# Attention's loop over head pairs in a fused two-layer kernel: a hardware loop written out as 32 iterations with constant waits

## What is computed

```
x = x + cross_attention(layernorm(x), ctx)      # 16 heads of 128, q and k normalised per head
x = x + hadamard_ffn(layernorm(x))              # 512 -> 2 x 2048 -> 512
x = x + state_space_mix(ctx, layernorm(x))      # scan over 512 values, 16 states
x = x + moe_ffn(layernorm(x))                   # 16 experts, two of them for each token, and a shared one
```

```
q = rmsnorm(xn @ Wq[:, h]) * gq;  k = rmsnorm(c @ Wk[:, h]) * gk;  v = c @ Wv[:, h]
out[:, h] = softmax(q @ k.T / sqrt(128)) @ v
x += out @ Wo
```

## Time and profile before

| | us |
|---|---|
| median of 3 runs | 2648.81 |
| lowest, highest | 2648.68, 2650.52 |
| span of the profiled execution, first to last instruction | 2643.4 |
| median less that span | 5.4 |
| attention in that span | 107.5 to 1272.9, behind a start of attention from about 80 |

### The profile page before, as it was taken

One profiled execution on the slowest core, in us unless ns is written; L12 is line 12 of the kernel. 1 busy time (PEld: TensorE's weight loads), 2 busy tenths in 40 slices (PEclk: granted clock), 3 DMA queues, 4 the chain that ended last, 5 costly groups with the idle time before them and its releaser, 6 DMA issues. The chain is left out here.

```text
span 2643.4 us, 35123 instructions
## 1 busy us (share of the span) xinstructions
PE 2284.0 (86%) x10784; PEld 1760.5 (67%) x10785; DVE 1797.4 (68%) x3239; ACT 1279.1 (48%) x2275; POOL 1356.7 (51%) x1104
## 2 busy tenths in 40 slices
PE   3699999999999999999693899998998869578980
PEld 2688888888887888887442666665665547456770
DVE  6466777768677777876683998898988966312323
ACT  2344454444454444544383866757766632223430
POOL 0232333323333333333293988989979941488324
PEclk8799999999999999999886999999999988789995
DMA  7513232122322232211348565555565321665317
GB/s 286 216 53 113 88 112 79 58 109 89 113 78 79 88 113 89 87 64 39 131 166 265 168 208 204 175 185 187 196 183 183 123 84 48 215 219 173 117 52 266
DMA packets 136761, 363.49 MB, mean 138 GB/s; under 512 B 21264, under 2 KB 58768, under 8 KB 118416
## 3 DMA queue, kind: packets, MB, share of 16 engines
q1 hardware_dynamic: 123504, 328.30, 36.1%
q0 software_dynamic: 6320, 20.71, 2.4%
q10 hardware_dynamic: 6768, 12.32, 1.2%
HBM read 289.99 MB, written 71.30 MB: 137 GB/s over the span
## 5 line engine op out<-in xcount | busy, mean ns | idle before, releaser
L641 POOL TENSOR_SCALAR att_probs<-att_probs,att_recip 128x512 f32<-128x512 f32 x256 | 181.8, 713 | 562.6 <-DVE att_recip L708 562.6
L1819 POOL TENSOR_TENSOR mix_drive<-mix_du,mix_rows 128x512 f32<-128x512 f32 x256 | 326.6, 1282 | 48.8 <-DVE mix_state L1891 15.9
L565 ACT ACTIVATE att_probs<-att_s,att_bias,att_rq 128x512 f32<-128x512 f32 x256 | 200.6, 784 | 288.3 <-DVE att_bias L704 288.1
L1891 DVE TENSOR_TENSOR_SCAN mix_state<-mix_state,mix_drive 128x512 f32<-128x512 f32 x256 | 312.9, 1222 | 30.8 <-POOL mix_drive L1819 17.3
L1671 ACT ACTIVATE mix_state<-mix_delta,mix_a 128x512 f32<-128x512 f32 x256 | 175.8, 690 | 227.8 <-DVE mix_drive L1902 187.4
L1804 POOL TENSOR_TENSOR mix_y<-mix_y,mix_drive 128x512 f32<-128x512 f32 x180 | 230.6, 1281 | 46.0 <-DVE mix_drive L1902 45.8
L1580 PE MATMUL mix_down<-mix_wd,mix_hT 128*128 128x512 f32 x512 | 232.0, 596 | 8.8 <-DVE residual_x L1922 8.8
L703 DVE TENSOR_REDUCE att_nmax<-att_s 128x1 f32<-128x512 f32 x256 | 175.1, 684 | 71.4 <-PE att_s L101 64.6
L744 DVE TENSOR_TENSOR att_pT<-att_pt,att_pT 128x512 fp32r<-128x512 f32 x256 | 170.1, 686 | 66.0 <-ACT att_pT L571 61.9
L571 ACT CAST att_pT<-att_pt 128x512 fp32r<-128x512 f32 x256 | 144.2, 593 | 133.4 <-PE att_pt L422 129.2
L99 PE MATMUL att_w<-att_w_qkv,att_cx 128*128 128x256 f32 x512 | 158.7, 310 | 35.2 <-DVE att_w_qkv L690 26.5
(11 more groups left out here) (354 smaller groups left out, 6703.7 us busy)
## 6 DMA issues: line engine op xcount, KB each, us to landing
att_xn<-normT SPq DMA_DIRECT2D x32, 2048.0 KB, 8.7
mix_gu<-guT SPq DMA_DIRECT2D x64, 1024.0 KB, 8.2
mix_rows<-bc_d SPq DMA_DIRECT2D x128, 256.0 KB, 4.8
guT<-att_ffnT SPq DMA_DIRECT2D x32, 512.0 KB, 5.7
mix_wd<-wdT SPq DMA_DIRECT2D x16, 1024.0 KB, 7.9
slots<-exp_y ACTq DMA_DIRECT2D x47, 256.0 KB
normT<-nrm_outT SPq DMA_DIRECT2D x4, 2048.0 KB, 9.1
exp_raw<-in_L_ffn_Wg SPq DMA_DIRECT2D x16, 512.0 KB, 5.1
```

The costliest lines, as they stand in the source:

```text
L565: act.activation(probs[:, n, :], ps_s[n % 2][:, :], ACT.Exp, bias=bias[:, n:n + 1], scale=rq[:, n:n + 1], accum_out=sums[:, n:n + 1]).then ...
L641: pool.tensor_scalar(probs[:, n, :], probs[:, n, :], recip[:, n:n + 1], 1.0, ALU.mult, ALU.mult).then_inc(s_pn, 1)
L1819: pool.tensor_tensor(drive[q % RING][:, :], du[i % DUS][:, :], rows[g % ROWS][:, 0, :], ALU.mult).then_inc(s_drive, 1)
L1891: dve.tensor_tensor_scan(h[:, :], h[:, :], drive[q % RING][:, :], 0.0, ALU.mult, ALU.add).then_inc(s_scan, 1)
```

## The change

Both loops are replaced by plain Python loops, so that the code of all 32 iterations stands one behind the other on every engine. `hp` is a number everywhere: the tests for the last pair become `hp < PAIRS - 1`, every wait compares with a constant, and the computation of the step counter's base falls away. On POOL `wait_apart(...)` becomes `pool.wait_ge(...)`, and `s_pace` goes. The instructions that compute, their order, the DMAs and what each waits for stay as they are.

```diff
         def pairs(eng, iteration):
-            with eng.Fori(0, PAIRS - 1) as hp:
+            for hp in range(PAIRS):
                 for b in range(B):
-                    iteration(hp, b, False)
-            for b in range(B):
-                iteration(PAIRS - 1, b, b == B - 1)
+                    iteration(hp, b, hp == PAIRS - 1 and b == B - 1)
...
-                    if b == 0 and not (isinstance(hp, int) and hp == PAIRS - 1):
+                    if b == 0 and hp < PAIRS - 1:
                         sp.wait_ge(s_w, 2 * hp + 2)
                         load_weights(hp + 1)
...
-                    if not (isinstance(hp, int) and b >= B - 2):
+                    if hp < PAIRS - 1 or b < B - 2:
...
                 def norm_p(i, n):
-                    wait_apart(pool, s_rec, 8 * i + n + 1, s_pace)
+                    pool.wait_ge(s_rec, 8 * i + n + 1)
...
-                base = own.n
-                per_pair = B * (8 + 1) + 3
-                def iteration(own, hp, b, last):
+                def iteration(hp, b, last):
                     i = hp * B + b
                     j = i + 1
-                    more = not isinstance(hp, int)
+                    more = hp < PAIRS - 1
...
-                with dve.Fori(0, PAIRS - 1) as hp:
-                    own = Steps(dve, s_dve, hp * per_pair + base)
-                    for b in range(B):
-                        iteration(own, hp, b, False)
-                    assert own.n == per_pair, own.n
-                own = Steps(dve, s_dve, (PAIRS - 1) * per_pair + base)
-                for b in range(B):
-                    iteration(own, PAIRS - 1, b, b == B - 1)
+                pairs(dve, iteration)
```

More of the change, by code:

```diff
@@ L303, in stage_attention @@
         s_dve = m.sem("dve_steps")
-        s_pace = m.sem("pace")
         s_fraw, s_ft, s_fout = m.sem("ffn_raw_in"), m.sem("ffn_turned"), m.sem("ffn_turned_out")
@@ L644, in norm_k @@
                 def norm_k(j):
-                    wait_apart(pool, s_kss, j + 1, s_pace)
+                    pool.wait_ge(s_kss, j + 1)
                     pool.tensor_tensor(rk[:, :], kss[:, :], power[:, :], ALU.pow).then_inc(s_rk, 1)
                 def norm_q(j):
-                    wait_apart(pool, s_qss, j + 1, s_pace)
+                    pool.wait_ge(s_qss, j + 1)
                     pool.tensor_tensor(rq[:, :], qss[:, :], power[:, :], ALU.pow).then_inc(s_rq, 1)
@@ L653, in split_ffn @@
                     parts = [fT[:, n, :, :].rearrange("p k n -> p (k n)") for n in range(2)]
-                    wait_apart(pool, s_fout, i + 1, s_pace)
-                    wait_apart(pool, s_fst, 16 * (i + 1), s_pace)
+                    pool.wait_ge(s_fout, i + 1)
+                    pool.wait_ge(s_fst, 16 * (i + 1))
                     pool.tensor_scalar(parts[0], fraw[:, :], 1.0, 1.0, ALU.mult, ALU.mult).then_inc(s_fhi, 1)
-                    wait_apart(pool, s_fhi, i + 1, s_pace)
+                    pool.wait_ge(s_fhi, i + 1)
                     pool.tensor_tensor(parts[1], fraw[:, :], parts[0].bitcast(F32), ALU.subtract).then_inc(s_flo, 1)
```

## The result

| | before | changed |
|---|---|---|
| median of the 4 runs each of the first comparison, us | 2649.02 | 2624.35 |
| lowest, highest | 2648.68, 2650.52 | 2621.90, 2629.47 |
| ratio, 95% interval | | 0.9914 [0.9897, 0.9932] |
| the same, two later comparisons | | 0.9903 [0.9888, 0.9919], 0.9908 [0.9893, 0.9922] |
| span of the profiled execution | 2643.4 | 2627.7 |

A forecast was written before the change was run, and what follows sets the result against it. Attention was taken as bound by TensorE (PE busy 97%), which stands for code at six loop jumps, 3.5 us each. Median 2648.8 less 21.2 gave 2627.6 us, range 2623 to 2633.

The forecast's parts named there:

- PE's two stands at each jump: In attention, PE waits on "issue" before `att_s` and before `att_w`, 6 times 1.5 us each, for a first and second code block.
- Iterations 1 to 30 sum to 1074.8: Attention written out: 1062.1 us undisturbed plus 12.7 for 10 lowered-clock iterations, against 1096.0 before; gain 21.2 us.
- the named unknown: How many attention iterations have the lowered clock: 10 of 30 may become 7 or 14, 3.8 us less to 5.1 more.
- Iteration 7's 38.09: Attention iteration ending with a jump, set against iteration 27, which ends without one and takes 35.36 us.
- the wait for the first exponential: Named with a low clock as the extra in attention's iteration 0 (39.13 us), which was taken to keep its time.
- stalls of 17.6 only: Lower bound of the gain: PE's "issue" waits alone, 17.6 us; central value 21.2.
- DVE's stand: DVE stands 2.3 us at its branch in attention, 6 times; hidden behind PE's stall and costed at nothing.
- Register waits and POOL's separate waits: In attention, register arithmetic was given nothing, 1 us in all; POOL's separate waits were called hidden, or a gain if not.
- 2648.8 - 21.2, all else unchanged: Median before less attention's gain gives 2627.6 us; the 5.4 us between profiled execution and median taken as unchanged.
- the fetches of rows 8 and 9: Profile rows of q8, TensorE's code queue: 3 packets in 11 us around a jump, 7 in the following 141 us.
- Rival 1, the experts' loop: Longer attention code shifts the experts' loop so its 21 jumps miss, about 3.5 us each: 2701 us; 5%.
- Rivals 2 and 3: 2: second stand isn't code and stays, 2638 us, 4%. 3: jump isn't the cost or its price returns, 2646 to 2650, 3%.

The follow-up runs named there:

- pe_mid_block: Kernel before with 100 needless transposes on TensorE and 25 needless memsets on DVE ahead of their kept loops; 2646.69 us, 0.9993 of before.
- shift40: Kernel before with 20 needless transposes (40 TensorE instructions) moving the head of TensorE's loop to a block's start; 2646.67 us, 0.9984 of before.
- both_held: Kernel before, loops kept, with 20 needless transposes on TensorE and 25 memsets on DVE moving both loop heads to a block's start; 2628.57 us, 0.9932.
- pe_only: Kernel before with TensorE's loop alone written out with constant waits, the other engines keeping theirs; 2646.60 us, 0.9989 of before.
- pe_out_dve_held: pe_only plus 25 needless memsets on DVE ahead of its kept loop; 2628.89 us, 0.9917 of before.
- pe_dve_out: pe_only with DVE's loop written out too; ACT, POOL and SP keep loops, register waits and POOL's separate waits; 2629.20 us, 0.9918 of before.
- all_but_pe: Changed kernel with TensorE's loop and register waits put back, all other engines written out; 2645.43 us, 0.9987 of before.
- dve_held: Kernel before with 25 needless memsets on DVE alone ahead of its loop, no transposes; 2648.75 us, 0.9997 of before.
- two_pairs: Kernel before with loops of 3 passes over two pairs each on all engines, pairs 6 and 7 written out behind; 2635.61 us, 0.9946 of before.

## Why the prediction was right, and where it was wrong

The time, the side and the range were right, and so was the cause of the gain, code fetched at a jump. The prediction saw it on TensorE alone; that DVE's fetch costs nearly as much when TensorE's is gone it had wrong. Point by point:

- *PE's two stands at each jump are two code blocks.* Right. One goes when the head is moved some 75 instructions away from a block's end (pe_mid_block), both when the body is held (shift40, both_held).
- *Iterations 1 to 30 sum to 1074.8.* Measured 1076.4: the base iteration was 35.33 instead of 35.40 (2.1 us less), the lowered clock came in 13 iterations instead of 10 (3.6 us more). That was the named unknown, within its bounds of 7 to 14.
- *The reading of the rows.* Two slips that change no sum. Iteration 7's 38.09 contains the lowered clock; beside iteration 27's 35.36 belongs an iteration without it, like 23 with 36.89. And iteration 0 doesn't hold the wait for the first exponential: PE is busy 38.72 of its 39.13 us, so what it has extra is the clock, 0.89. The range adds its parts loosely: stalls of 17.6 only and 5.1 of clock would end at 2637, not 2633.
- *DVE's stand: "were it to stay, DVE with 25 to 29 busy of 35.4 us would still absorb it, so I cost this at nothing on either side."* Wrong, and the step that failed. With TensorE's fetches gone and DVE's left, PE waited 14.7 us for `att_probs` and 2.3 us were gained (pe_only); with DVE's gone too, 20.7 (pe_out_dve_held). Idle time over an iteration says nothing about a delay at one point of a chain with two score banks. The sum survived, by luck, only because the change removes that stand as well. As a forecast for TensorE's loop alone the same reasoning would have said 20 us, and 2 came.
- *Register waits and POOL's separate waits: nothing, 1 us in all.* Perhaps too small, not settled. With them left on ACT, POOL and SP 4.9 us are missing by the medians (pe_dve_out), with all of them kept 4.3 (both_held), neither clear of noise. My row for it, iterations 28 to 30, still had POOL's separate waits, so it was not quite the changed form.
- *2648.8 - 21.2, all else unchanged.* The closeness is in part luck. Iterations 1 to 30 gave 19.7 us (1096.0 - 1076.4), the medians moved by 24.7, and the other 5 lie outside them. What comes behind iteration 29 took 1436.6 to 1439.1 us in the three profiles of the changed kernel and 1441.1 to 1443.7 in those of pe_only, all_but_pe, shift40, dve_held, pe_mid_block and two_pairs, though only 1436.1 in before's. So part may lie in the later stages, whose code is the same; why isn't shown.
- *"A body of 1634 matmuls and loads would stay resident ... the fetches of rows 8 and 9 speak against that."* The doubt about the room was wrong; the fetches have another reason. The Trainium skill, "Runtime: NRT & Kernel Launch", section Instruction fetch mechanics, gives TensorE 2048 instructions in blocks of 256, and shift40's empty q8 agrees: 8 blocks, if the 1751 instructions and the block fetched ahead fit. In before's trace 17 TensorE records lie between the branch and the second stand, so the head lay about that far ahead of a block's end. The body then touched 8 blocks, and a ninth, fetched ahead, displaced the first; the 9 packets in a pass agree. That it is 8 with the one ahead, and not 7 without it, no run here tells apart. The same section's two blocks fit neither TensorE's held body nor DVE's, which is 343 instructions long in blocks of 8 KB.
- *Rival 1, the experts' loop.* It did not come. With 8 blocks held a body of some 150 instructions can't lose its own target, so 5% was too much for it; the branch's median stayed at 215 ns in the changed kernel and, at another place, at 208 in shift40's.
- *Rivals 2 and 3.* Excluded by the changed kernel's waits of PE, which have no "issue" left, and by its time.

## What to carry to other kernels

A backward jump of a hardware loop is nearly free or costs about 3 to 3.5 us here (17.7 us for six of DVE's, pe_only less pe_out_dve_held; 21.1 for six of TensorE's, all_but_pe less the changed kernel). By the account above, which of the two depends on how many code blocks the body touches. So look in the trace for the fetches, not at the loop: at the code queues and at waits on "issue" behind the jump. The branch's duration tells only on TensorE (3378 ns against 208). DVE's own is nearly as short in before, where it then stands 2.3 us, as in dve_held (median 56 ns), where it doesn't:

```profile
L841 DVEq COMPARE_BRANCH  x7: 55/63/72, 255.8 to 1135.5; - x7
```

Before writing a loop out, moving its head by a few instructions may give most of it: 45 padding operations gave some 20 of 25 us. It is fragile: with 80 more transposes (pe_mid_block) the gain was gone. When all engines jump at one time, their stands hide each other: an experiment on one engine alone shows almost none of the gain, and says nothing about the pair.

## What the runs showed of the hardware that I had not expected

- With its head moved by 40 instructions TensorE held a loop body of 1751 instruction records and fetched nothing (no q8 block in 850 us); at its old place the same body was fetched again in every pass (53 blocks).
- DVE held 343 instructions or not in the same way (q14: 29 blocks of 8 KB, or none), by a shift of 25.
- The loops of ACT (198 records, branch 45 ns) and POOL (152) were held in both_held: q14 brought nothing between 250 and 1100 us while they turned. They were tried at no other place.
- The lowered clock came in 13 of 30 iterations instead of 10 with the same work in each, at 1.2 to 1.3 us apiece; over all profiles it is 7 (pe_mid_block) to 13 of iterations 1 to 29. That alone moves a time by several microseconds.
